# Heads of chunks 1 and 3 in other PSUM banks, in a fused retention and channel-mix block

## What is computed

```
h = layernorm(x) * (1 + ca) + sa
q, k = rotary(h Wq), rotary(h Wk)        # 8 heads of 64
v, g = h Wv, h Wg                        # 8 heads of 128
scores = q k^T * 64^-0.5 * decay(head, t - s), causal, no softmax
o = scores v, each head normalised over its 128 values, * gn_weight + gn_bias
x = x + ga * ((o * silu(g)) Wo)
h = layernorm(x) * (1 + cb) + sb
x = x + gb * sigmoid(hr W_r) * (relu(hk W_k)^2 W_v)     # hr, hk: h mixed with the token before
```

## Time and profile before

| | |
|---|---|
| median of 3 runs | 769.83 us (768.88 to 770.64) |
| the profiled execution: its time | 768.16 us |
| its span, first to last instruction | 766.4 us |
| mean granted TensorE clock | 0.984 |
| PE busy | 737.5 us, 96% |
| PE weight loads busy | 649.7 us, 85% |
| DVE busy | 606.3 us, 79% |
| POOL busy | 587.1 us, 77% |
| ACT busy | 452.4 us, 59% |

### The profile page before, as it was taken

How to read it: one execution, slowest core, us unless ns; L and a number is a source line. 1 busy time by engine, 2 the same in 40 slices (tenths; PEclk the granted TensorE clock), 3 DMA queues, 4 the chain that set the end, 5 groups by cost and what they waited for, 6 DMA issues and landing times.

```text
span 766.4 us, 29026 instructions
## 1 busy us (share of the span) xinstructions
PE 737.5 (96%) x12093; PEld 649.7 (85%) x12093; DVE 606.3 (79%) x1283; ACT 452.4 (59%) x819; POOL 587.1 (77%) x641
## 2 busy tenths in 40 slices
PE   5788999999999999999999999999999999999996
PEld 3577888888988888888888888888888888888875
DVE  6978777888878788887878878797887878786545
ACT  4234555656565565656556565656656565656664
POOL 3746787897878888798878987788887987777641
PEclk9889999999999999999999999999999999999998
DMA  9422211121223132122313212231321222122100
GB/s 327 123 51 50 44 39 38 41 43 34 47 51 71 23 72 49 40 55 43 71 30 71 43 30 65 50 70 24 71 45 35 65 43 57 23 58 43 37 15 29
DMA packets 66402, 42.46 MB, mean 55 GB/s; under 512 B 38232, under 2 KB 55904, under 8 KB 66272
## 3 DMA queue, kind: packets, MB, share of 16 engines
q1 hardware_dynamic: 65552, 39.81, 22.3%
q10 hardware_dynamic: 720, 0.80, 0.3%
HBM read 11.22 MB, written 4.20 MB: 20 GB/s over the span
## 4 chain that ended last, share of the span: by engine, by line
PE 86%; DVE 8%; issue 3%; ACT 1%; POOL 1%; DMA 1%; ACTq 0%; DVEq 0%; POOLq 0%
PE ring L280 48%; PE O_E L280 14%; PE outs L280 13%; PE ring L295 7%; PE O_O L280 3%; DVE N L916 1%; PE ring L319 1%; DVE gn_sum L909 1%; DVE h_full L845 1%; DVE turned L860 1%; DVE swapped L865 1%; DMA wmod<-in_w_mod 1%; ACT N L619 1%; DVE sin_k L882 1%; DVE rot_k L879 1%
## 5 line engine op out<-in xcount | busy, mean ns | idle before, releaser
L1145 POOL TENSOR_TENSOR y<-y,gate 128x512 f32<-128x512 f32 x123 | 155.1, 1282 | 24.7 <-ACT y L631 24.7
L280 PEld LDWEIGHTS outs<-wo_gated,y 128*128 128x128 f32 x992 | 127.7, 191 | 10.2 <-POOL y L1145 1.7
L1128 POOL TENSOR_TENSOR rot_k<-rot_k,sin_k 128x256 f32<-128x256 f32 x128 | 108.5, 868 | 34.1 <-DVE sin_k L882 34.1
L280 PE MATMUL outs<-wo_gated,y 128*128 128x128 f32 x992 | 131.3, 275 | 1.1 <-POOL y L1145 1.0
L909 DVE TENSOR_REDUCE gn_sum<-N 128x4 f32<-128x512 f32 x128 | 81.9, 681 | 48.6 <-ACT N L619 48.5
L1138 POOL TENSOR_TENSOR gn_rstd<-gn_var,minus_half 128x8 f32<-128x8 f32 x64 | 105.4, 1646 | 5.0
L1122 POOL TENSOR_TENSOR qT<-qT,swapped 128x512 f32<-128x512 f32 x64 | 83.2, 1300 | 19.8 <-DVE swapped L865 19.6
L631 ACT ACTIVATE y<-ring,gn 128x512 f32<-128x512 f32 x126 | 91.0, 777 | 4.8 <-PE ring L295 4.8
L600 ACT ACTIVATE v_odd<-ring 128x512 f32<-128x512 f32 x64 | 38.4, 599 | 92.2 <-PE ring L280 92.2
L889 DVE TENSOR_TENSOR A<-ring,consts 128x256 f32<-128x256 f32 x128 | 48.0, 417 | 50.9 <-PE ring L280 50.9
L903 DVE TENSOR_TENSOR S<-ring,S 128x512 f32<-128x512 f32 x112 | 76.9, 686 | 1.9
(11 more groups left out here) (149 smaller groups left out, 2101.9 us busy)
## 6 DMA issues: line engine op xcount, KB each, us to landing
v<-v_odd SPq DMA_DIRECT2D x128, 128.0 KB, 2.3
k_odd<-rot_k SPq DMA_DIRECT2D x128, 64.0 KB, 2.2
X<-in_x SPq DMA_DIRECT2D x16, 256.0 KB, 3.4
out<-X SPq DMA_DIRECT2D x15, 256.0 KB, 3.2
key_tables<-in_const SPq DMA_DIRECT2D x7, 256.0 KB, 8.3
rotary_q<-in_const_q SPq DMA_DIRECT2D x2, 512.0 KB, 8.3
gates<-stored_rows SPq DMA_DIRECT2D x8, 128.0 KB, 3.2
N<-in_w_qkT SPq DMA_DIRECT2D x1, 512.0 KB, 4.7
```

What stands on the lines that cost most here:

```text
L280: return e.matmul(o, lhsT, rhs, start=start, stop=stop, skip_group_check=True)
L1128: done = e.tensor_tensor(turned[:, n, :, :], turned[:, n, :, :], sin[:, n, :, :], op)
L1145: e.tensor_tensor(y[:, n % NY, :], y[:, n % NY, :], gate[:, n % 2, :], ALU.mult).then_inc(sem["y"])
```

## The change

Chunks 1 and 3 (`SPARE`) accumulate their even heads in the `outs` bank and their odd heads in a ring bank, the first or the last of the ring, that `hold_heads` takes out of the ring when `attend` of the chunk is written. `free_heads` gives it back at the end of the same step, to be released by `norm_heads`. `attend`, `recall`, `square` and `norm_heads` take their banks from `heads_of(i)`. The wait of `attend(i)` is now for the last earlier chunk in the same pair of banks (`banks_before`): chunk 1 for none, chunk 2 for chunk 0, chunk 3 for chunk 1, chunk 4 for chunk 2, from chunk 5 on for the chunk before, as it was. `project_out` waits at the head of each group for `norm_heads(3)`, once. While a bank is held `take_bank` chooses among the other four. `EARLY` is not used.

```diff
+        held = set()
+        SPARE = (1, 3)
+
+        def heads_of(i):
+
+            return (by(PAIRS, out_bank[:, :]), by(PAIRS, bank_of["heads", i])) if i in SPARE else [o[:, :, :] for o in O]
+
+        def banks_before(i):
+
+            return max((j + 1 for j in range(i) if (j in SPARE) == (i in SPARE)), default=0)
+
...
-                first = min(range(RING + 1 - adjoining), key=lambda n: sorted(taken[n:n + adjoining], reverse=True))
+                ready = [n for n in range(RING + 1 - adjoining) if not held & set(range(n, n + adjoining))]
+                first = min(ready, key=lambda n: sorted(taken[n:n + adjoining], reverse=True))
...
+            def hold_heads(i):
+
+                ends = (0, RING - 1)
+                n = min(ends, key=lambda n: taken[n])
+                for name, value in released.get(n, ()):
+                    at.wait_ge(name, value)
+                held.add(n)
+                bank_of["heads", i] = ring[:, n, :]
+
+            def free_heads(i):
+                for n in sorted(held):
+                    released[n] = (("n_O", i + 1),)
+                    taken[n] = max(taken) + 1
+                held.clear()
...
             def attend(i):
 
+                if i in SPARE:
+                    hold_heads(i)
+                heads = heads_of(i)
                 for eo in "EO":
-                    at.wait_ge("n_" + eo, i)
+                    at.wait_ge("n_" + eo, banks_before(i))
                     at.wait_ge("A_" + eo, i + 1)
...
             def project_out(n):
                 g, h = divmod(n, H)
                 if h == 0:
+                    at.wait_ge("n_E", max(SPARE) + 1)
                     at.wait_ge("residual", g)
...
                     project_k(i)
+                for i in due(step - 1, 1, 4, 3):
+                    free_heads(i)
+                for i in due(step - 1, 1, 2, 1):
+                    free_heads(i)
             project_r(LAST - 1)
```

More of the change, by code:

```diff
@@ L27 @@
 MID = T // 2
+EARLY = 5
 NX, NHT, NQ, NN, NY, NS = 7, 4, 2, 2 * GC, 4, 3
@@ L398, in attend @@
                             rows = halves(half ^ odd)
-                            done = matmul(O[odd][halves(half), n, :], A[rows, odd, n, :], v[rows, i % 2, odd, n, :],
+                            done = matmul(heads[odd][halves(half), n, :], A[rows, odd, n, :], v[rows, i % 2, odd, n, :],
                                           n == 0, False)
@@ L410, in recall @@
                         for odd in range(2):
-                            done = matmul(O[odd][halves(half), n, :], queries(i, odd, n, half), before[halves(odd), :],
+                            done = matmul(heads[odd][halves(half), n, :], queries(i, odd, n, half), before[halves(odd), :],
                                           False, n == PAIRS - 1)
@@ L618, in square @@
                 at.wait_ge("nT_psum", PAIRS * ((i - NN) // GC + 1))
-                e.activation(N[:, i % NN, odd, :, :], O[odd][:, :, :], ACT.Square).then_inc(sem["sq_" + eo])
+                e.activation(N[:, i % NN, odd, :, :], heads_of(i)[odd], ACT.Square).then_inc(sem["sq_" + eo])
             def gate_silu(n):
@@ L915, in norm_heads @@
                 rstd = gn_rstd[:, i % 2, odd, :].unsqueeze(2).broadcast_to([P, PAIRS, V])
-                e.tensor_tensor(N[:, i % NN, odd, :, :], O[odd][:, :, :], rstd, ALU.mult).then_inc(sem["n_" + eo])
+                e.tensor_tensor(N[:, i % NN, odd, :, :], heads_of(i)[odd], rstd, ALU.mult).then_inc(sem["n_" + eo])
             def residual(g):
```

## The result

The changed kernel takes 763.4 us (median of 5 runs, 762.48 to 764.74) beside 768.88 us for the kernel before (766.57 to 770.64): a ratio of 0.9931, with a 95% interval of 0.9906 to 0.9956, so 3.4 to 7.2 us faster. Two more comparisons, with 14 and 17 runs of the kernel before, gave 0.9943 (0.9930 to 0.9957) and 0.9936 (0.9920 to 0.9951). The gain is 4.3 to 5.5 us. Forecast were a gain of 5.5 us and a median of 764.3.

What follows compares the result with a forecast made beforehand. PE was taken to bound the kernel, with DVE next in steps 2 to 4. Gains of 5.2 us up to mask(5) and 0.3 us in the middle, 5.5 together, off 769.83 gave 764.3 us; range 761.8 to 768.4.

Steps and rivals of the forecast that it cites:

- The bound: Steps 2 to 4: PE's three waits before attend, 4.97 us, and slow clock behind them, about 5 us; DVE late next.
- Steps 2 and 3: Scores and squares ready before DVE needs them, so no DVE idle time is left; mask(4)'s turn at 60.45.
- Step 4: Chunk 4 transposes wait for full_h(2), a 1.8 us gap; 1.66 us charged for a slow stretch, 1.06 of DVE idle.
- Step 5: Chunk 5 transposes wait for rotate_k(6) until 69.10; mask(5) at 71.07 against 76.27, a gain of 5.2 us.
- The middle: Six waits for rotate_k, steps 12 to 52, go (1.7 us); 28 other steps lose 0.05 each (1.4); net gain 0.3.
- The clock does not come back: Steps 2 to 5 each still have a slow stretch; 3.6 us or so of the gain goes, 767.9 us; chance 0.18.
- A ring of four: Bank takes waiting for DVE cost 1.7 us a step over three steps; only 0.3 us gained, 769.5 us; chance 0.10.
- The slower ring: Key transposes of 28 steps wait for rotate_k, 0.35 us each; 2.9 us slower, 772.7 us; chance 0.07.

Runs made afterwards that it cites:

- filled: Kernel before, with identity matmuls ahead of the waits of attend, five for chunks 1 and 2, eight for chunk 3; waits stay: 763.86 us beside 767.17, 0.9963.
- the one with only the ring's order: Changed kernel with all heads back in O_E and O_O and the old waits; a ring bank taken out unused in steps 2 and 4: 768.1 us beside 767.34.
- the one with the waits put back: Changed kernel, banks and ring kept, but attend of every chunk waits again for norm_heads of the chunk before: 767.16 us beside 767.34.
- only chunk 1 elsewhere: Changed kernel with only chunk 1 in other banks; chunk 2 waits for chunk 0, chunk 3 for chunk 2: 764.62 us beside 767.34, 0.9962.
- the overfilled kernel: Kernel before, with ten identity matmuls ahead of each wait of attend of chunks 1, 2 and 3; waits stay: 767.53 us beside 767.34.

## Why the prediction was right

**The bound.** That PE's waits and the clock behind them are the loss of steps 2 to 4, and that DVE is late next, holds: the waits are gone, DVE is busy through these steps. A slow stretch cost less than the 1.66 us that were read from PE alone: filled, steps 2 to 4 (the last up to the transposes of step 5) are shorter by 10.27 - 8.90 = 1.37, 10.23 - 8.86 = 1.37 and 13.37 - 11.90 = 1.47 us.

**Steps 2 and 3.** Forecast were key transposes at 40.43, 48.19 and 57.07 (the scores' 58.33 less 1.26) in steps 2 to 4; measured 40.79, 48.32 and 57.57. Counted from step 2, 7.76 and 16.64 against 7.53 and 16.78 us. The wait for `full_h(2)`, with a gap of 1.8 us, is there with 1.60. In step 3 DVE idles for 0.38 us, where no idle time was forecast.

**Step 4.** This term was mis-sized: "a gap of 1.8 us lies among those that were followed by a slow stretch, so I charge 1.66". None followed in any of the five traces that have this gap alone, and filling it brought nothing. Slow stretches stood behind three waits out of three in the kernel before and in the one with only the ring's order, and behind one out of three with the waits put back; there, and with only chunk 1 elsewhere, it came in step 4, where a wait of `attend` of 0.78 us stands right behind the gap. Why the gap alone is not followed by one stays open. Without the charge the sum was 6.26 us at `mask(5)`; measured are 76.27 - 70.50 = 5.77, or 6.13 counted from step 2.

**Step 5.** The new wait for `rotate_k(6)` is there, 0.84 us. One loss was not foreseen: the time from these transposes to those of step 6 is 11.00 us where it was 10.42, 0.58 us more. Part of it is a pause of PE in the middle of `state(5)`, where the program has no wait and the profile names no instruction that it waits for:

```profile
71.94 0.32 PE L308 MATMUL ring<-v,rot_k 64*64 64x128 f32 x1 [0.21 <-issue]
```

All three traces of the changed kernel have the loss (11.00, 11.22 and 11.06 us); with the gap of step 4 filled it is not there (10.37). Its cause stays open.

**The middle.** Forecast was a net gain of 0.3 us: the six waits of the earlier trace rows gone, small costs at 28 steps. The changed kernel is 5.25 us ahead at the transposes of step 6, 6.01 at step 52 and 5.43 at step 63: 0.2 net. The six waits no longer stand among the waits of the weight loads. The lead grows by 0.25 to 0.30 us at each of the steps 12, 20, 28, 36, 44 and 52, which the forecast had named, 1.66 us together where 1.7 were forecast. Transposes of steps 51 and 52, before and after:

```profile
585.68 0.41 PE L295 MATMUL ring<-consts,rot_k 64*128 64x64 f32 x8
596.76 0.46 PE L295 MATMUL ring<-consts,rot_k 64*128 64x64 f32 x8
...
579.97 0.46 PE L323 MATMUL ring<-consts,rot_k 64*128 64x64 f32 x8
590.75 0.41 PE L323 MATMUL ring<-consts,rot_k 64*128 64x64 f32 x8
```

In most of the other steps the lead shrinks by some hundredths of a us, together by 1.66 - 0.18 = 1.48 us where 1.4 were forecast. That it is transposes waiting for `rotate_k` that lose them is not shown: the profile lists no such wait.

**The rivals.** *The clock does not come back* fell: it was 1.0 from 40 to 76 us in every trace of the changed kernel. (Its price was slightly off: the idle times named come to 4.92 us, of which 1.06 were charged already, so 3.86 would go and not 3.6.) The Trainium skill, "TensorE: Matmul & The Clock Gate", section "What's actually happening", puts the ramp penalty, for modelling, under 1% of a typical kernel's span and advises not to fit it to a specific count of slow matmuls; the trace agrees with the size, 4.21 us of 766.4 or 0.55%. The prediction's sum with no slow stretch counted was 1.6 us; the two kernels without slow stretches, the filled one and the changed one, differ by 29.66 - 27.68 = 1.98 us between steps 2 and 5, so as a forecast for equal clocks it was near. For this change it left out the larger part, those 4.21 us in the profiled executions. *A ring of four* was right in kind: the ring's new order costs 0.86 to 1.33 us from step 2 to step 5. Another bank for chunk 3 wins 0.93 us there by removing the wait of step 5. *The slower ring* fell: no wait for `rotate_k` is listed in the middle, and the lead is 0.2 us larger at its end.

**The median.** The sum of 5.5 us matched the first comparison to a tenth; the two larger comparisons gave 4.3 to 4.9. The match to a tenth is in part luck, since errors with opposite signs lie in the sum: the charge of step 4 made the gain too small; the loss in step 5 that was not foreseen, and the three slow stretches of one execution taken for the usual number, made it too large.

## What to carry to other kernels

Where PE has short waits, look at what its clock does behind them: here the slow stretches cost as much as the waits did, and more in the profiled execution, and filling the waits with useless matmuls that fit into them brought two thirds to three quarters of the gain without touching what is waited for. Measure first how long such matmuls take: ten of them took back all that the clock gave. When a buffer is taken out of a shared ring, follow the whole order of the ring, since the next user may land on the buffer that is emptied last; another choice of buffer was worth 1.1 to 1.8 us here. And a loss that comes and goes between executions is not to be read from one profile.

## What the runs showed of the hardware

The same wait of 1.40 us in front of `attend` of chunk 1 was followed by a stretch at a granted clock of 0.50 (1.2 GHz) in the kernel before and in the one with only the ring's order, and by none in the one with only the waits put back. The last two differ up to there only in the bank that the waiting matmul writes; whether the bank has a part in it is not shown. A gap of 1.57 to 1.61 us ahead of the key transposes of step 4 was followed by none in five traces. In the overfilled kernel the ten identity matmuls of 128x128 32-bit numbers took about 2.5 us at a granted clock of 1.0 and show as 20 rows in the trace.
